# Row maxima twenty steps ahead, handed over in blocks, and reciprocals on a 128x16 tile, in an attention and expert-routing layer

## The reference, cut to what matters

```python
xn = layernorm(x)                                   # (4, 2048, 512)
q = (xn @ Wq).reshape(B, S, 4, 4, 32)               # 4 key heads, 4 query heads on each
k, v = (xn @ Wk), (xn @ Wv)                         # (B, S, 4, 32)
scores = einsum('bqkgd,bskd->bkgqs', q, k) * scale  # causal mask
attn = softmax(scores); out = einsum('bkgqs,bskd->bqkgd', attn, v) @ Wo
# experts: 32 of them, 6 for each token, at most 96 tokens an expert
act = silu(xb @ gate) * (xb @ up); yb = act @ w_down   # gathered rows xb, weighted and summed
# and one shared expert for all tokens
```

## Time and profile before

| | |
|---|---|
| profiled execution | 3644.07 us, its span 3642.0 us |
| mean granted TensorE clock | 0.993 |
| PE, DVE, ACT, POOL busy | 97%, 65%, 45%, 57% of the span |
| stage_a, stage_m, stage_b, stage_c begin at | 0, 1133, 1428, 3460 us |

### The profile page before, as it was taken

One profiled execution on the slowest core, in us unless ns is written; L12 is line 12 of the kernel. 1 busy time (PEld: TensorE's weight loads), 2 busy tenths in 40 slices (PEclk: granted clock), 3 DMA queues, 4 the chain that ended last, 5 costly groups with the idle time before them and its releaser, 6 DMA issues. The chain is left out here.

```text
span 3642.0 us, 56595 instructions
## 1 busy us (share of the span) xinstructions
PE 3547.0 (97%) x19904; PEld 2213.6 (61%) x19904; DVE 2363.1 (65%) x5390; ACT 1629.3 (45%) x3347; POOL 2058.3 (57%) x1592
## 2 busy tenths in 40 slices
PE   7999999999997999999999999999999999999999
PEld 5888888888875555555555555555555555554387
DVE  6455555554543445877787787778778777876244
ACT  3232222222221113656566565666656566666711
POOL 0333323323332222877877787787778778778700
PEclk9999999999998999999999999999999999999999
DMA  5333333332238995102202211220221121020086
GB/s 175 102 110 101 101 110 101 101 113 97 101 122 231 286 316 147 44 24 56 50 14 58 53 32 35 56 50 13 56 54 34 35 53 43 23 68 12 19 303 241
DMA packets 228173, 340.55 MB, mean 94 GB/s; under 512 B 65088, under 2 KB 75968, under 8 KB 227968
## 3 DMA queue, kind: packets, MB, share of 16 engines
q1 hardware_dynamic: 197232, 307.77, 27.7%
q0 software_dynamic: 17920, 12.82, 1.7%
q10 hardware_dynamic: 12816, 17.33, 1.3%
HBM read 217.15 MB, written 120.35 MB: 93 GB/s over the span
## 5 line engine op out<-in xcount | busy, mean ns | idle before, releaser
L1390 ACT ACTIVATE prb<-sps 128x512 f32<-128x512 f32 (+3 forms) x2481 | 1155.1, 540 | 734.0 <-PE sps L1500 694.5
L1413 DVE TENSOR_REDUCE mx<-mps 128x1 f32<-128x512 f32 x1440 | 939.9, 681 | 161.5 <-PE mps L1477 161.4
L1325 POOL TENSOR_TENSOR rows<-rows,prb 128x1024 f32<-128x1024 f32 x372 | 881.8, 2394 | 0.0
L396 POOL DMA_INDIRECT tab_s<-pay,slot x384 | 378.0, 984 | 732.7 <-DVE tokf L694 481.0
L1416 DVE CUSTOM_DVE_ANT_0 mps<-mps,bias 128x256 f32<-128x256 f32 (+1 forms) x960 | 489.5, 523 | 212.3 <-PE mps L1477 212.0
L1518 PE MATMUL ops<-prb,vst 128*32 128x512 f32 (+3 forms) x5120 | 598.7, 539 | 6.0 <-POOL prb L1310 4.4
L1319 POOL TENSOR_TENSOR rows<-prb 128x1024 f32<-128x1024 f32 x192 | 455.1, 2392 | 151.6 <-ACT prb L1390 151.6
L1477 PE MATMUL mps<-x_lo,w_lo 96*128 96x512 f32 (+2 forms) x1280 | 487.4, 387 | 8.9 <-DVE mx L1413 3.3
L1500 PE MATMUL sps<-w_hi,x_hi 97*128 97x512 f32 (+2 forms) x1280 | 483.0, 389 | 9.8 <-ACT prb L1390 8.0
L1500 PE MATMUL sps<-w_lo,x_lo 97*128 97x512 f32 (+2 forms) x1201 | 447.4, 389 | 5.9 <-ACT prb L1390 5.9
L751 PE MATMUL acc<-x_hi,w_hi 128*128 128x512 f32 x1088 | 430.2, 395 | 6.0 <-DVE qk_lo L596 6.0
(11 more groups left out here) (178 smaller groups left out, 4256.6 us busy)
## 6 DMA issues: line engine op xcount, KB each, us to landing
wgu<-in_e_gu SPq DMA_DIRECT2D x24, 1408.0 KB, 9.2
rows<-in_x SPq DMA_DIRECT2D x16, 1024.0 KB
xn_s<-rows SPq DMA_DIRECT2D x16, 1024.0 KB, 5.1
y_sb<-in_x SPq DMA_DIRECT2D x16, 1024.0 KB
q_hi_s<-qk_hi SPq DMA_DIRECT2D x16, 1024.0 KB
q_lo_s<-qk_lo SPq DMA_DIRECT2D x16, 1024.0 KB
base<-y_sb SPq DMA_DIRECT2D x16, 1024.0 KB
w_hi<-q_hi_s SPq DMA_DIRECT2D x64, 256.0 KB, 4.4
```

The costliest lines, as they stand in the source:

```text
L396: nc.gpsimd.indirect_dma_start(t["tab"], bass.IndirectOffsetOnAxis(ap=slot[:, i, k:k + 1], axis=0), pay[:, i, k, :], None, bounds_check=E ...
L1325: nc.gpsimd.tensor_tensor(acc4, acc4, prb[:, (2 * n + pr) % RP], ALU.add).then_inc(add_done, 1)
L1390: nc.scalar.activation(prb[:, (2 * k + h // 2) % RP, h % 2, q0:CH], bank(bg, GROUP * k + h)[:, q0:CH], ACT.Exp, scale=SCALE).then_inc(exp_ ...
L1413: V.tensor_reduce(mx[:, h * NKT + qt, j:j + 1], mps[:, n % R, 0:wr], AX.X, ALU.max).then_inc(mred_done, 1)
```

## The change

- The pieces of a group now run over its own steps 0 to 19 and steps 20 to 39 of the group before (`AHEAD = 20`), in all 40 steps, with 0.75 of a share in steps with r of 2 or 3. Stage_m computes 84 pieces of group 0 instead of 160, over experts 0 to 30, two or three at an expert's start in a row. Group 15 computes its last 76 pieces in its own steps 0 to 19, and uses six banks from step 21 on.
- The maxima are handed over chunk by chunk: DVE negates 16 columns, turns them itself, and ACT starts four DMAs for each chunk, two steps after the chunk's last piece: 16 DMAs a group. PE waits for them at the first step of each chunk. The last pieces of the four chunks are computed in steps 23 and 30 of the group before and 3 and 19 of the own.
- The denominators: SP writes one row of each head to DRAM (4 DMAs), waits, reads them back as 128x16, DVE inverts that seven steps after the chunk's last, SP writes it to DRAM, waits, and reads it back into 32 partitions for each head (4 DMAs). POOL multiplies ten steps after the last. Stage_c's own last chunk is inverted as before.
- Q and K of group 1 are loaded at the start of stage_b, no longer during stage_m.
- In group 15 only the fours that begin at step 24 or later have 4 adds; C0 is 24.

```diff
+AHEAD = 20
+def maxima_by_step():
+    steps, pieces = attention_steps(), maxima_pieces()
+    order = [(k + len(steps) - AHEAD) % len(steps) for k in range(len(steps))]
+    room = [0.75 if steps[k][2] >= 2 else 1.0 for k in order]
+    cost = [64 + piece[5] for piece in pieces]
...
+def negate_block(dve, att, mred, c):
+    n = c % JC
...
+    dve.wait_ge(att["mred_done"], mred)
+    V.tensor_reduce(neg[:, c % 2, 0:GROUP * NT].rearrange("p (h q) -> p h q", q=NT),
+                    mx[:].rearrange("p (h q) j -> p h q j", q=NKT)[:, :, n * NT:(n + 1) * NT, :], AX.X,
+                    ALU.max, negate=True).then_inc(att["neg_done"], 1)
+    dve.wait_ge(att["neg_done"], c + 1)
+    if c >= 2:
+        dve.wait_ge(att["c_in"], 16 * NT * (c - 1))
+    V.transpose(negt[:, c % 2, :].bitcast(F32), neg[:, c % 2, :].bitcast(F32)).then_inc(att["turned"], 1)
+def maxima_row(act, att, p, c):
+    n = c % JC
+    act.wait_ge(att["turned"], c + 1)
+    act.wait_ge(att["c_in"], 16 * NT * c)
+    for x in range(NT):
+        row = att["qst"][p][R3:R3 + 1, n, :, :].rearrange("o h (q x r) -> o (h q) x r", x=NT, r=HD)
+        act.dma_start(row[:, :, x, :].bitcast(F32),
+                      att["negt"][HD * x:HD * x + GROUP * NT, c % 2, :].bitcast(F32)).then_inc(att["c_in"], 16)
...
-                if n % NQ == 0 and n > 3 * NQ:
-                    load_qk(sp, t, att, 0, 1, n // NQ - 4)
...
+            def denominators(n):
+                q = n % JC % 2
+                sp.wait_ge(den_done, n + 2)
+                for h in range(GROUP):
+                    sp.dma_start(t["den"][q, h:h + 1], den[q][HD * h:HD * h + 1, :]).then_inc(den_out, 16)
+                sp.wait_ge(den_out, 16 * GROUP * (n + 1))
+                sp.dma_start(dsm[q][:], t["den"][q].rearrange("h (c e) -> (h c) e", e=EL)).then_inc(dsm_in, 16)
+            def reciprocals(n):
+                q = n % JC % 2
+                sp.wait_ge(rsm_done, n + 1)
+                sp.dma_start(t["rec"][q].rearrange("h (c e) -> (h c) e", e=EL), rsm[q][:]).then_inc(rec_out, 16)
+                sp.wait_ge(rec_out, 16 * n + 16)
+                for h in range(GROUP):
+                    sp.dma_start(rden[q][HD * h:HD * (h + 1), :],
+                                 t["rec"][q, h:h + 1].to_broadcast([HD, CH])).then_inc(rden_in, 16)
+            def blocks(i, p):
+                n = (2 * i + p) * JC
+                if n:
+                    denominators(n - 1)
+                    reciprocals(n - 1)
+                denominators(n)
+                if n:
+                    store((n - 1) // JC // 2, (n - 1) // JC % 2, JC - 1)
+                reciprocals(n)
+                store(i, p, 0)
+                for j in range(1, JC - 1):
+                    denominators(n + j)
+                    reciprocals(n + j)
+                    store(i, p, j)
             sp.sem_inc(att_out, 16)
+            for c in range(JC):
+                load_qk(sp, t, att, 0, 1, c)
             load_v(sp, t, att, 0, 1)
             for i in range(BG // 2 - 1):
                 for p in range(2):
-                    for j in range(JC - 1):
-                        store(i, p, j)
+                    blocks(i, p)
                     for c in range(JC):
                         sp.wait_ge(s_done, (2 * i + p) * NU + GROUP * (lasts[-2] + 1 + NT * (c + 1)))
                         load_qk(sp, t, att, i + 1, p, c)
                     sp.wait_ge(pv_done, (2 * i + p) * NK + NK + 8)
                     load_v(sp, t, att, i + 1, p)
-                    store(i, p, JC - 1)
...
-            def invert(bg, j, part):
-                if part == 0:
-                    dve.wait_ge(den_done, bg * JC + j + 2)
-                cols = slice(part * P, (part + 1) * P)
-                V.reciprocal(rden[j % 2][:, cols], den[j % 2][:, cols]).then_inc(rden_done, 1)
+            def invert(bg, j):
+                dve.wait_ge(dsm_in, 16 * (bg * JC + j + 1))
+                V.reciprocal(rsm[j % 2][:], dsm[j % 2][:]).then_inc(rsm_done, 1)
...
+                if kt == 0 and h == 0:
+                    pe.wait_ge(c_in, 16 * NT * (JC * bg + j + 1))
```

More of the change, by code:

```diff
@@ L860, in maxima_pieces, with attention_steps, block_ends @@
     return pieces
+def attention_steps():
+    steps = [(j, kt, kt - JC * j) for j in range(JC) for kt in range(JC * (j + 1))]
+    return [(j, kt, r if r >= 0 else -1) for j, kt, r in steps]
+AHEAD = 20
[4 more added lines that the diff above has]
+    cost = [64 + piece[5] for piece in pieces]
+    first = []
+    for x in range(len(steps)):
+        share = sum(room[:x]) / sum(room) * sum(cost)
+        first.append(sum(1 for n in range(len(pieces)) if sum(cost[:n + 1]) <= share + 1))
+    return first + [len(pieces)]
+def block_ends():
+    return [max(n for n, piece in enumerate(maxima_pieces()) if piece[1] // NT == c) for c in range(JC)]
+def negate_block(dve, att, mred, c):
+    n = c % JC
+    V = dve
+    neg, negt, mx = att["neg"], att["negt"], att["mx"]
+    dve.wait_ge(att["mred_done"], mred)
[14 more added lines that the diff above has]
+                      att["negt"][HD * x:HD * x + GROUP * NT, c % 2, :].bitcast(F32)).then_inc(att["c_in"], 16)
 def carried_to_b(nc, ctx, car):
@@ L1012, in _ @@
                 nc.scalar.activation(sil[n % 2][:], gps[0:CAP, 0:I], ACT.Silu).then_inc(sil_done, 1)
[L1013 to L1018, removed]
+                for c, end in enumerate(ends):
+                    if n and end in quota(n - 1):
+                        maxima_row(act, att, 0, c)
                 if n < E - 1:
@@ L1145, in _ @@
                         down(e - 1, k)
[L1146 to L1148 removed]
+                assert len(todo) <= R
             turn_hidden(E - 1)
@@ L1227, in stage_b, with maxima @@
         NM = len(pieces)
-        MI = NM + 1
-        M1 = 37
-        work = [1.0 * (CH - max(r, 0) * P) + (1.1 if steps[k - LAG][2] < 0 else 1.6) *
-                (CH - max(steps[k - LAG][2], 0) * P) + CH for k, (j, kt, r) in enumerate(steps)][:M1]
-        for k in range(M1):
-            if any(k - LAG - 1 - part in lasts for part in range(NT)) or LAG <= k < LAG + NT:
-                work[k] -= 400
-        cost = [64 + piece[5] for piece in pieces]
-        def upto(k):
-            share = sum(work[:k]) / sum(work) * sum(cost)
-            return sum(1 for n in range(NM) if sum(cost[:n + 1]) <= share + 1)
-        first = [upto(k) for k in range(M1)] + [NM] * (NK - M1 + 1)
-        def quota(k):
-            return range(first[k], first[k + 1])
-        MFIN = M1
+        ends = block_ends()
+        first = maxima_by_step()
+        def maxima(bg, k):
+            if k >= NK - AHEAD:
+                x = k - (NK - AHEAD)
+                return [(bg + 1, n) for n in range(first[x], first[x + 1])] if bg < END else []
+            x = k + AHEAD
+            return [(bg, n) for n in range(first[x], first[x + 1])]
         block = ctx.enter_context(nc.Block())
@@ L1283, in _ @@
                          ).then_inc(car["a_ld0"], 16)
-            for j in range(JC - 1):
-                store(BG // 2 - 1, 1, j)
+            blocks(BG // 2 - 1, 1)
         @block.gpsimd
@@ L1510, in output @@
                     pe.wait_ge(num_done, bg * JC + j + 1)
-                if bg < END:
-                    direct, opens = r >= 0, r == 0 and j <= 1
-                else:
-                    direct, opens = r >= 0 or kt % 4 == 3, kt == (3 if j else 0)
+                alone = any(k == f + 3 and direct(bg, gi) for gi, f in enumerate(fours))
+                opens = r == 0 and j <= 1 or alone and kt == 3
                 if opens:
```

203 lines of the change are left out of this document (91 added, 112 removed).

## The result

Six runs of the changed kernel have a median of 3628.24 us (3623.59 to 3631.67), six of the kernel before 3640.61 (3639.99 to 3648.52): ratio 0.996, 95% interval 0.9949 to 0.9971. That is 12 us won where 63 were forecast, and outside the forecast's range. The change is clear of the noise and small. The profiled executions differ by more, 3644.07 and 3625.24 with spans of 3642.0 and 3623.5: the first lay 3.5 over its median, the second 3.0 under.

What follows compares the result with a forecast made beforehand. PE was taken to bound the groups, at its pace except for 6.9 us of lateness each. Groups -55, stage_m -16, group 15 +12 and -4 sum to -63: median 3640.4 to 3577 us, range 3534 to 3618.

Steps and rivals of the forecast that it cites:

- Groups 0 to 14: Attention groups: spread pieces and small reciprocals remove most of PE's lateness, 3.7 us a group, -55 us in 15 groups.
- (a): Attention, ACT's steps 25, 32, 5 and 21: 16 DMA issues at 0.47 us delay exponentials, costing 0.3 us a group.
- rival B: Groups keep their lateness: ACT's issuing and POOL's adds take back DVE's gain; 1 us won a group, 3617 us; chance 0.17.
- Steps 37 to 39: End of a group: pieces now fill these steps, where scores waited for ACT to empty a bank; gain 1.7 us.
- The small pieces: Eight small masked pieces, moved from steps 0 and 1 to step 20 of the group before, cost the same 1.15 us.
- (b): Attention, step 36: POOL's adds before the masks make it late for PE, costing 1.0 us a group.
- (d): Attention: the reciprocals' way through DRAM, tightest at a group's start, makes DVE late at step 10, costing 0.5 us a group.
- rival D: Slower: landings on the way through DRAM take 4.4 us, DVE and PE wait 5.4 us a group; 3664 us; chance 0.08.
- Stage_m: Expert stage: fewer pieces leave PE at 8.15 us an expert, but POOL's scatter chain holds it at 8.75; -16 us.
- rival A: Stage_m runs at PE's pace because scatter landings shorten once on the path; -31 for -16, 3562 us; chance 0.13.
- Group 15: Last group: +12 us from 76 pieces in steps 0 to 19, -4 us from step 20 to the end.
- DVE's splits beside POOL's adds: Group 15, adds of steps 26 on: both engines slow together, each add gives up 0.42 us, five of them 2 us.

Runs made afterwards that it cites:

- sp_rows: The changed kernel with SP instead of ACT issuing each chunk's four DMAs of maxima in the attention stage; 3594.2 us, ratio 0.9833 to the kernel before.
- sp_m_none: sp_rows with stage_m's pieces of maxima left out on PE and DVE, the first 84 maxima taken as 0; 3566.22 us, ratio 0.9784 to the kernel before.
- recip_dve: The changed kernel with DVE inverting the denominators in four pieces of 128x128 again, nothing sent through DRAM; 3666.05 us, ratio 1.0028 to the kernel before.
- act_twice: The changed kernel with a second DMA of the same source, into spare DRAM, behind each of ACT's four; 3911.31 us, ratio 1.0707 to the kernel before.

## Why the prediction was wrong

**Groups 0 to 14: -55 forecast, -11 measured, by one term.** The step that failed is (a), the price of ACT's sixteen DMAs, 0.3 us a group with bounds 0 and 7.5. sp_rows takes just this term out and has groups of 124.65; 128.37 - 3.7 is 124.67. Its ratio of 0.9833 (0.981 to 0.9857) makes 3580 us of 3640.6 (3571 to 3589), where the forecast was 3577. The term measured 3.0, ten times its price, for reasons that the rows show. An issue takes 0.51 to 0.61 us and a row of four 2.43, where one issue's 0.47 had been taken four times; that alone moves the next exponential of a full step from 0.2 late to 0.76 late (1.27 behind the first score in group 2 against 0.51 in sp_rows). The half microsecond of room that I gave the fourth score was not there: in group 2 it came 1.92 behind the first, against 1.17, so 0.75 late too. So a plain row of 2.43 us lengthens its step by all that it delays: in the groups where nothing else happens step 25 takes 4.22 to 4.25 us against 3.48 to 3.50 in sp_rows, step 32 4.02 to 4.06 against 3.17 to 3.19, step 5 3.02 to 3.06 against 2.55. That is 2.1 of the 3.0. The other 0.9 come from eleven of 62 rows that took 0.3 to 1.3 us more still, seven of them in step 25 of every second group (see the last section), and from three falls of the clock. The prediction had neither. The reading "ACT is busy only 78 of 128 us" used against rival B was the misleading one. A share of busy time says nothing about the 1.7 us between two exponentials, and PE has just three banks to bridge them.

Rival B had the mechanism for ACT and was given 0.17; its other half, POOL's adds, did not happen. Its 1 us a group was nearly right (0.73): its -23 stands against the -18.5 of the profiled executions. The groups make -4 of the difference, group 15 makes 2.4 and stage_a, which B left out, -1.2; the rest is stage_m.

**The other terms of the groups.** Steps 37 to 39 gave 1.63 for 1.7. The small pieces kept their 1.15. Term (b), POOL late at step 36, 1.0: nothing, 0.05 us in steps 37 to 39. Term (d), the way through DRAM, 0.5, and with it rival D: nothing. The small writes and reads landed in 1.4 to 2.0 us from their issue, and DVE never stood idle before a reciprocal:

```profile
L1489 DVE RECIPROCAL rsm<-dsm 128x16 f32<-128x16 f32 x59 | 13.9, 236 | 0.0
...
y_sb<-rec_s SPq DMA_DIRECT2D x236, 64.0 KB, 2.0
...
dsm<-den_s SPq DMA_DIRECT2D x59, 8.0 KB, 1.6
rec_s<-rsm SPq DMA_DIRECT2D x59, 8.0 KB, 1.4
```

A reciprocal of 128x16 takes 0.236 us, not an eighth of 0.95. What (b) and (d) gave back went to lateness that I had forecast to go: 0.59 stay in step 2, where PE waits for ACT's copy of the outputs (0.34 before), and 0.5 in steps 9 and 10 (0.44 before). That sp_rows comes out at the forecast's 3.7 is partly luck, because these errors cancel.

The Trainium skill (DMA: Bandwidth & Descriptors, "Anatomy of one DMA — SWDGE (gpsimd) path") gives about 2 us and warns of more for a target in HBM. Its figure is for DMAs that GpSimd issues, and these are SP's; they landed in 1.4 to 2.0. No run here shows the long case, though one of them (the reciprocals' write) goes to DRAM and took 1.4.

**Stage_m: -16 forecast, -16.8 measured, by a wrong reason.** I had the chain of scatters hold PE at 8.75 us an expert, and PE alone at 8.15. PE alone is 8.42, and in these 32 experts the chain holds PE up by 0.7 us in all even at 7.90. Where the scatters do wait for their landings, in sp_m_none, they are 8.3 apart and not 8.75: the 7.3 us to landing count from the start of the issue, so that the issue's 1.44 was counted twice, and from a landing to the next issue some 0.9 us pass. And 8.15, in the forecast as in rival A, took the expert's own work from the last one (7.56), which has no next expert's rows to turn; with them it is 7.90. The -16.8 is 32.9 - 16.2 = 16.7 us of pieces on PE, and that the forecast had the same number is luck. At 8.42 an expert, bringing Q and K later keeps some 6 us from coming back. At before's 9.0 it seems to win nothing, since the experts there take just PE's own time; no run tried it alone.

**Group 15: +8 forecast, +10.4 measured.** Steps 0 to 19 took 58.7 for 46.7, the +12 of the forecast. In the second part the stall of 4.38 at step 22 is gone, but that part as a whole became only 1.6 us shorter where 4 were forecast; which of its terms fell short was not tried. Its term for DVE's splits beside POOL's adds can be read from the timelines of the kernel after (three adds one by one, then three splits):

```profile
3400.87 2.38 POOL L1388 TENSOR_TENSOR rows<-prb 128x1024 f32<-128x1024 f32 x1 [2.22 <-ACT prb L1454]
...
3406.01 2.83 POOL L1394 TENSOR_TENSOR rows<-rows,prb 128x1024 f32<-128x1024 f32 x1
3408.80 2.84 POOL L1394 TENSOR_TENSOR rows<-rows,prb 128x1024 f32<-128x1024 f32 x1
...
3399.35 0.69 DVE L1497 TENSOR_TENSOR w_hi<-wo,w_hi 128x512 fp32r<-128x512 f32 x1
...
3408.36 1.04 DVE L1501 TENSOR_TENSOR w_hi<-x_hi,w_hi 128x512 fp32r<-128x512 f32 x1 [1.76 <-ACT w_hi L1443]
3410.82 1.37 DVE L1501 TENSOR_TENSOR w_hi<-x_hi,w_hi 128x512 fp32r<-128x512 f32 x1 [1.43 <-ACT w_hi L1443]
```

The split of 3399.35 meets no add and takes 0.69. The other two end at 3409.40 and 3412.19, each 0.55 us behind the end of an add (3408.84 and 3411.64): a split that starts beside an add waits until the add is over and then runs. All 15 splits that met POOL's work in the two kernels end so, 0.54 to 0.56 us behind the end of one of its instructions. The add that follows takes 2.83 instead of 2.38, so a split costs POOL 0.45 us. The prediction read the same rows as both engines slowed together; they take turns, by whole instructions. That is what the Trainium skill (SBUF — State Buffer, "SBUF: two separate sides") says, and the trace agrees. What was wrong was the price put on it, 6 x 2.2 = 13 us: the 2.2 of a split is for the most part its own waiting, and POOL gives up 6 x 0.45 = 2.7, near the 2 of the sum.

## What to carry to other kernels

A DMA issue held ACT for 0.51 to 0.61 us here, and a row of them in front of work that feeds PE is priced by the time until the next bank is needed, not by that engine's share of busy time. Put such issues on an engine whose time nobody waits for (SP here), or one behind each instruction of the stream. When a list of waits and transfers on SP grows, look at what stands at its end: here loads that came late and piled up in front of an unrelated 32 KB row cost 2.7 us a group, more than the small reciprocals won (0.8). And when two engines slow each other down, look at the ends of single instructions, not at sums: waiting in turn and running slower look the same in a sum.

## What the runs showed that was not expected

- **Long issues and instruction packets.** In the attention stage of the kernel after ACT issued 62 rows of four DMAs. The last three of a row took 1.89 to 1.91 us in 48 of them, 1.98 to 2.03 in three, and 2.17 to 3.15 in eleven. In all eleven a packet of the queue called q8 instruction lies over the one issue that is long, and that issue ends 0.34 to 0.38 us behind the packet's end, whether the packet took 0.92 us or 1.45. In none of the 48 does such a packet lie. The DMA view of the row at 1869.31:

```profile
q8 instruction: 1, 0.02, 2.5%
```

  The 13 long issues of recip_dve end 0.37 to 0.39 us behind such a packet, and of the eight on SP in sp_rows seven end 0.36 to 0.39 behind one. So the issue waits for the packet to arrive; whose instructions it carries, and why a DMA's issue waits for them, stays open. The packets come every 20 us or so, in step with the groups: seven of the eleven fall on step 25 of groups 1, 3, 5 and so on up to 13, which is why the groups of the kernel after are uneven. The Trainium skill (Runtime: NRT & Kernel Launch, "Instruction fetch mechanics") holds that crossing such a block is mostly hidden. Here it was not hidden from an engine that was issuing DMAs: 0.3 to 1.3 us each, 8.1 us in all.
- **The clock.** In the 15 groups of the kernel after waits of PE of 1.45, 1.61 and 1.83 us were each followed by 3.4 us at the lower level (granted clock 0.50). Waits of 1.48 and 1.73 us were not, nor was any under 1.4 but one of 0.86 at the very start of the stage. In act_twice waits of up to 3.9 us, four a group, brought the mean to 0.93.
- **DVE's turn of 128x32** (the four that replaced PE's transpose and ACT's copy) takes 0.21 us; PE waits for none of them.
